# A decoder's last stage, FP4 feed-forward: three of its steps are placed on other engines and another memory

## The reference

```python
def fp4_quant_dequant(x):                       # _GRID 0 .5 1 1.5 2 3 4 6
    xb = x.reshape(shape[:-1] + (shape[-1] // BLOCK, BLOCK))
    scale = jnp.max(jnp.abs(xb), axis=-1, keepdims=True) / 6.0
    scale = jnp.maximum(scale, jnp.float32(1e-12))
    xn = xb / scale
    idx = jnp.searchsorted(_MID, jnp.abs(xn))
    q = _GRID[idx] * jnp.sign(xn) * scale
    return q.reshape(shape)
...
xl = _layernorm(x)                              # per token, 128 features
gate = fp4_linear(xl, w_gate)                   # 128 -> 352
y = fp4_linear(xl, w_up)                        # 128 -> 352
x = x + fp4_linear(jax.nn.silu(gate) * y, w_down)   # 352 -> 128
```

## Time and profile before

| | |
|---|---|
| time, median of 3 runs | 3627.68 us (3622.21 to 3630.7) |
| the profiled execution's own time | 3633.43 us |
| its span | 3631.6 us |
| mean granted TensorE clock over the span | 0.929 of full |
| busy over the span: PE, PEld, DVE, ACT, POOL | 3202.6, 2343.7, 2524.3, 2207.0, 1508.8 us |
| last stage's main block, first instruction to last of DVE | 3255.4 to 3621.4 us |

### The profile page before, as it was taken

One profiled execution on the slowest core, in us unless ns is written; L12 is line 12 of the kernel. 1 busy time (PEld: TensorE's weight loads), 2 busy tenths in 40 slices (PEclk: granted clock), 3 DMA queues, 4 the chain that ended last, 5 costly groups with the idle time before them and its releaser, 6 DMA issues. The chain is left out here.

```text
span 3631.6 us, 96279 instructions
## 1 busy us (share of the span) xinstructions
PE 3202.6 (88%) x27249; PEld 2343.7 (65%) x27249; DVE 2524.3 (70%) x7783; ACT 2207.0 (61%) x8571; POOL 1508.8 (42%) x2416
## 2 busy tenths in 40 slices
PE   8999999899999999999999731887996999977776
PEld 4656565788888888888888520665664666644444
DVE  7888888676777777777767640114666888879997
ACT  6888888566666666666666300334776999962221
POOL 6888888111111111111111125004654777746665
PEclk9999999999999999999999855999998999986666
DMA  4000000000000000000000101321000000000000
GB/s 138 0 0 0 0 0 1 4 2 3 2 2 2 2 2 2 2 2 2 2 2 2 70 9 50 84 77 30 17 16 5 6 5 5 6 3 6 12 12 18
DMA packets 80357, 54.27 MB, mean 15 GB/s; under 512 B 24801, under 2 KB 74413, under 8 KB 80160
## 3 DMA queue, kind: packets, MB, share of 16 engines
q1 hardware_dynamic: 76192, 45.27, 4.4%
q0 software_dynamic: 4096, 8.16, 0.8%
HBM read 32.67 MB, written 20.97 MB: 15 GB/s over the span
## 5 line engine op out<-in xcount | busy, mean ns | idle before, releaser
L785 DVE COPY b_prT<-b_tr 128x512 f32<-128x512 f32 x512 | 352.4, 688 | 324.3 <-PE b_tr L694 320.6
L930 POOL TENSOR_TENSOR b_ln_var<-b_ln_mean_var,all_eps 128x1 f32<-128x1 f32 x64 | 12.2, 190 | 1158.5 <-DVE b_ln_mean_var L129 1158.5
L883 ACT ACTIVATE b_pr<-b_sc,b_low 128x205 f32<-128x205 f32 x1024 | 431.2, 431 | 40.9 <-DVE b_low L761 40.9
L467 ACT ACTIVATE a_pr<-a_sc,a_low 128x128 f32<-128x128 f32 x1024 | 365.5, 384 | 36.4 <-POOL a_pn L511 26.2
L776 DVE TENSOR_SCALAR b_pn<-b_pr,b_rec 128x205 f32<-128x205 f32 x1024 | 291.6, 327 | 54.7
L694 PE MATMUL b_tr<-all_ident,b_pn 128*128 128x128 f32 x2048 | 322.4, 280 | 6.2 <-DVE b_prT L785 2.5
L2064 ACT ACTIVATE f_pr<-f_sc,f_low 128x77 f32<-128x77 f32 x1024 | 320.3, 338 | 10.2 <-DVE f_low L1955 2.9
L502 POOL TENSOR_TENSOR a_kx<-a_qk,w_hsel 128x512 f32<-128x512 f32 x256 | 291.8, 1151 | 2.4 <-DVE a_qk L338 2.4
L694 PEld LDWEIGHTS b_tr<-all_ident,b_pn 128*128 128x128 f32 x2048 | 226.5, 141 | 92.2 <-issue 69.5
L254 PE MATMUL a_sc<-a_kx,a_qk 128*128 128x512 f32 x512 | 261.9, 593 | 0.0
L761 DVE TENSOR_REDUCE b_low<-b_sc 128x4 f32<-128x820 f32 x256 | 256.3, 1001 | 6.0 <-PE b_sc L682 6.0
(11 more groups left out here) (290 smaller groups left out, 8651.3 us busy)
## 6 DMA issues: line engine op xcount, KB each, us to landing
scratch_x<-r_zeros SPq DMA_DIRECT2D x12, 512.0 KB, 5.0
e_xr<-scratch_x SPq DMA_DIRECT2D x24, 256.0 KB, 3.0
scratch_y<-e_yr SPq DMA_DIRECT2D x24, 256.0 KB, 2.4
all_X<-in_x SPq DMA_DIRECT2D x8, 512.0 KB, 7.0
e_w<-in_e_w SPq DMA_DIRECT2D x16, 256.0 KB, 3.0
out_x<-all_X SPq DMA_DIRECT2D x8, 512.0 KB, 3.2
w_mask<-in_mask SPq DMA_DIRECT2D x1, 2464.0 KB, 9.8
b_cT<-in_ctxT SPq DMA_DIRECT2D x32, 77.0 KB, 1.9
```

The lines of the kernel that those rows point to most:

```text
L467: op = act.activation(pr[:, u % 2, g], sc[:, u % 2, 128 * g:128 * g + 128], ACT.Exp, bias=low[:, u % 2, g:g + 1], scale=-1.0, accum_out=su ...
L785: dve.tensor_copy(prT[:, j % 2, i].rearrange("p h t q -> p (h t q)"), tr[:]).then_inc(prT_made, 1)
L883: op = act.activation(pr[:, j % 2, g, 0:KN], sc[:, j % 2, h, KN * i:KN * i + KN], ACT.Exp, bias=low[:, j % 2, g:g + 1], scale=-1.0, accum_ ...
```

## The change

It touches the last stage only (and adds three memsets of small constants on DVE at the kernel's start).

- One PSUM bank `pf` is allocated to the rounding: `v` and one tensor `t` for each of fx and fh lie in it. `t` takes the block maxima (k = 0) and then, in place, the reciprocals (k = 2). `v` is k = 3's output. `fp4_step` has five steps (`FP4_STEPS = 5`); k = 4, `power`, reads v from PSUM and writes SBUF. `scale` stays in SBUF.
- `magic` is formed on ACT by `fp4_magic`, in two dependent activations: Relu(power x M - M), then Identity(. + M), with M = 1.5 x 2^22, bias taken from a [128, 1] constant.
- `sum` stays on DVE as `fp4_sum`, at the end of the step, behind a wait for ACT's magic (`magic_done`).
- `norm_apply` leaves DVE: ACT's `normalise` computes xn = x * rstd + shift in one activation (bias and scale both [128, 1] operands), and POOL's `norm` computes, beside variance + eps and the power, `minus_mean` and `shift` = -mean x rstd: four instructions in the place of two.
- ACT's step is now, in order: copy_xT(b+2), gate(b+2), normalise(b+4), copy_hT(b-1), fp4_magic of fx for b+3, fp4_magic of fh for b. In the prologue it does normalise and fp4_magic of sequences 0 to 3 first, then copy_xT and gate of 0 and 1.
- In `fp4_weights` the magic constants are made on ACT likewise.

```diff
@@ -2145,25 +2145,26 @@
 
 FP4_SHRINK = 1.0 - 2.0 ** -24
 FP4_MAGIC = 1.5 * 2.0 ** 22
-FP4_STEPS = 7
+FP4_STEPS = 5
 EXPONENT_BITS = 0x7F800000
 
 class Fp4Buffers:
 
-    def __init__(self, mem, name, n):
-        nb = n // QB
-        self.amax = mem.sbuf(f"{name}_amax", [128, nb])
+    def __init__(self, mem, name, v, t):
+        n, nb = v.shape[1], t.shape[1]
+        self.v, self.t = v, t
         self.scale = mem.sbuf(f"{name}_scale", [128, 2, nb])
-        self.rscale = mem.sbuf(f"{name}_rscale", [128, nb])
-        self.v = mem.sbuf(f"{name}_v", [128, n])
         self.power = mem.sbuf(f"{name}_power", [128, n])
         self.magic = mem.sbuf(f"{name}_magic", [128, 2, n])
         self.sum = mem.sbuf(f"{name}_sum", [128, 2, n])
         self.rounded = mem.sbuf(f"{name}_rounded", [128, n])
         self.q = mem.sbuf(f"{name}_q", [128, 2, n])
         self.steps = mem.sem(f"{name}_steps")
+        self.magic_done = mem.sem(f"{name}_magic_done")
+        self.sum_done = mem.sem(f"{name}_sum_done")
         self.round_done = mem.sem(f"{name}_round_done")
         self.q_done = mem.sem(f"{name}_q_done")
 
@@ -2180,32 +2181,53 @@
 
     if k == 0:
-        if due(b - 1):
-            dve.wait_ge(f.q_done, b - 1)
-        op = dve.tensor_reduce(f.amax[:], blocks(x), AX.X, ALU.max, apply_absolute_value=True)
+        if due(b):
+            dve.wait_ge(f.steps, FP4_STEPS * b)
+        op = dve.tensor_reduce(f.t, blocks(x), AX.X, ALU.max, apply_absolute_value=True)
     else:
         dve.wait_ge(f.steps, FP4_STEPS * b + k)
     if k == 1:
-        op = dve.tensor_scalar(f.scale[:, p], f.amax[:], 1.0 / 6.0, 1e-12, ALU.mult, ALU.max)
+        if due(b - 1):
+            dve.wait_ge(f.q_done, b - 1)
+        op = dve.tensor_scalar(f.scale[:, p], f.t, 1.0 / 6.0, 1e-12, ALU.mult, ALU.max)
     if k == 2:
-        op = dve.reciprocal(f.rscale[:], f.scale[:, p])
+        op = dve.reciprocal(f.t, f.scale[:, p])
     if k == 3:
-        op = dve.tensor_tensor(blocks(f.v[:]), blocks(x), per_block(f.rscale[:]), ALU.mult)
+        if due(b):
+            dve.wait_ge(f.sum_done, b)
+        op = dve.tensor_tensor(blocks(f.v), blocks(x), per_block(f.t), ALU.mult)
     if k == 4:
-        op = dve.tensor_scalar(f.power[:].bitcast(U32), f.v[:].bitcast(U32), EXPONENT_BITS, None, ALU.bitwise_and)
-    if k == 5:
-        op = dve.tensor_scalar(f.magic[:, p], f.power[:], 1.0, FP4_MAGIC, ALU.max, ALU.mult)
-    if k == 6:
-        op = dve.scalar_tensor_tensor(out=f.sum[:, p], in0=f.v[:], scalar=FP4_SHRINK, in1=f.magic[:, p],
-                                      op0=ALU.mult, op1=ALU.add)
+        if due(b):
+            dve.wait_ge(f.magic_done, 2 * b)
+        op = dve.tensor_scalar(f.power[:].bitcast(U32), f.v.bitcast(U32), EXPONENT_BITS, None, ALU.bitwise_and)
     op.then_inc(f.steps, 1)
+def fp4_magic(act, f, consts, b, p):
+    act.wait_ge(f.steps, FP4_STEPS * b + FP4_STEPS)
+    if due(b - 1):
+        act.wait_ge(f.round_done, b - 1)
+    act.activation(f.magic[:, p], f.power[:], ACT.Relu, bias=consts.magic[:, 0:1], scale=FP4_MAGIC)\
+        .then_inc(f.magic_done, 1)
+    act.wait_ge(f.magic_done, 2 * b + 1)
+    act.activation(f.magic[:, p], f.magic[:, p], ACT.Identity, bias=consts.magic[:, 1:2]).then_inc(f.magic_done, 1)
+def fp4_sum(dve, f, b, p):
+    if due(b - 1):
+        dve.wait_ge(f.round_done, b - 1)
+    dve.wait_ge(f.magic_done, 2 * b + 2)
+    dve.scalar_tensor_tensor(out=f.sum[:, p], in0=f.v, scalar=FP4_SHRINK, in1=f.magic[:, p], op0=ALU.mult,
+                             op1=ALU.add).then_inc(f.sum_done, 1)
 
 def fp4_round(eng, f, b, p, q_read):
 
     if due(b):
         eng.wait_ge(f.q_done, b)
-    eng.wait_ge(f.steps, FP4_STEPS * b + FP4_STEPS)
+    eng.wait_ge(f.sum_done, b + 1)
     eng.tensor_tensor(f.rounded[:], f.sum[:, p], f.magic[:, p], ALU.subtract).then_inc(f.round_done, 1)
     if due(b - 1):
         eng.wait_ge(q_read, b - 1)
@@ -2246,8 +2268,14 @@
         gu_made, gated_done, h_done = mem.sem("gu_made"), mem.sem("gated_done"), mem.sem("h_done")
         hT_made, hT_copied = mem.sem("hT_made"), mem.sem("hT_copied")
         y_made, y_added, stored = mem.sem("y_made"), mem.sem("y_added"), mem.sem("stored")
-        fx, fh = Fp4Buffers(mem, "fx", D), Fp4Buffers(mem, "fh", GI)
+        pf = mem.psum("pf", [128, 512])
+        nx, nh = D // QB, GI // QB
+        fh = Fp4Buffers(mem, "fh", pf[:, 0:GI], pf[:, GI + D:GI + D + nh])
+        fx = Fp4Buffers(mem, "fx", pf[:, GI:GI + D], pf[:, GI + D + nh:GI + D + nh + nx])
         ln = NormBuffers(mem, "ln")
+        shift = mem.sbuf("shift", [128, 2])
+        minus_mean = mem.sbuf("minus_mean", [128, 2])
+        shift_done = mem.sem("shift_done")
 
@@ -2302,6 +2330,13 @@
 
             @block.scalar
             def _(act):
+                def normalise(b, p):
+                    if due(b - 1):
+                        act.wait_ge(fx.steps, FP4_STEPS * (b - 1) - 1)
+                    act.wait_ge(shift_done, b + 1)
+                    act.activation(ln.xn[:, p], X[:, b], ACT.Identity, bias=shift[:, p:p + 1],
+                                   scale=ln.rstd[:, p:p + 1]).then_inc(ln.xn_done, 1)
                 def copy_xT(b):
                     if due(b):
                         act.wait_ge(gu_made, b)
@@ -2326,9 +2361,19 @@
                     if inside(b + 2):
                         copy_xT(b + 2)
                         gate(b + 2, p)
+                    if inside(b + 4):
+                        normalise(b + 4, p)
                     if inside(b - 1):
                         copy_hT(b - 1)
-
+                    if inside(b + 3):
+                        fp4_magic(act, fx, consts, b + 3, 1 - p)
+                    if inside(b):
+                        fp4_magic(act, fh, consts, b, p)
+                for b in range(4):
+                    normalise(b, b % 2)
+                    if b < 3:
+                        fp4_magic(act, fx, consts, b, b % 2)
                 for b in (0, 1):
                     copy_xT(b)
                     gate(b, b)
@@ -2365,32 +2410,48 @@
                             residual(b - 2)
                     if inside(b + 1):
                         product(b + 1, 1 - p)
-                    if inside(b + 4):
-                        norm_apply(dve, ln, X[:, b + 4], b + 4, p)
+                    if inside(b + 3):
+                        fp4_sum(dve, fx, b + 3, 1 - p)
+                    if inside(b):
+                        fp4_sum(dve, fh, b, p)
 
                 for b in range(4):
                     norm_statistics(dve, ln, X[:, b], b, b % 2)
                     norm_moments(dve, ln, b % 2)
-                    norm_apply(dve, ln, X[:, b], b, b % 2)
                     if b < 3:
                         dve.wait_ge(ln.xn_done, b + 1)
                         for k in range(FP4_STEPS):
                             fp4_step(dve, fx, ln.xn[:, b % 2], b, b % 2, k)
+                        fp4_sum(dve, fx, b, b % 2)
                 product(0, 0)
                 over_sequences(dve, step, **steps)
 
             @block.gpsimd
             def _(pool):
+                def norm(b, p):
+                    if due(b - 1):
+                        pool.wait_ge(ln.xn_done, b - 1)
+                    pool.wait_ge(ln.moments_done, b + 1)
+                    pool.tensor_tensor(ln.var_eps[:, p:p + 1], ln.mv[:, p, 1:2], consts.eps[:, 0:1], ALU.add)\
+                        .then_inc(ln.eps_added, 1)
+                    pool.tensor_tensor(minus_mean[:, p:p + 1], ln.mv[:, p, 0:1], consts.minus_one[:, 0:1], ALU.mult)
+                    pool.wait_ge(ln.eps_added, b + 1)
+                    pool.tensor_tensor(ln.rstd[:, p:p + 1], ln.var_eps[:, p:p + 1], consts.minus_half[:, 0:1], ALU.pow)\
+                        .then_inc(ln.rstd_done, 1)
+                    pool.wait_ge(ln.rstd_done, b + 1)
+                    pool.tensor_tensor(shift[:, p:p + 1], minus_mean[:, p:p + 1], ln.rstd[:, p:p + 1], ALU.mult)\
+                        .then_inc(shift_done, 1)
                 def step(b, p, last):
                     if inside(b + 4):
-                        norm_rsqrt(pool, ln, consts, b + 4, p)
+                        norm(b + 4, p)
                     if inside(b + 3):
                         fp4_round(pool, fx, b + 3, 1 - p, xT_made)
                     if inside(b):
                         fp4_round(pool, fh, b, p, hT_made)
 
                 for b in range(4):
-                    norm_rsqrt(pool, ln, consts, b, b % 2)
+                    norm(b, b % 2)
                     if b < 3:
                         fp4_round(pool, fx, b, b % 2, xT_made)
                 over_sequences(pool, step, **steps)
@@ -2399,7 +2460,8 @@
 def fp4_weights(nc, mem, raw, wT, wdT, consts):
 
     NW = 3 * 128
-    fp4 = Fp4Buffers(mem, "w", NW)
+    pf = mem.psum("pf", [128, 512])
+    fp4 = Fp4Buffers(mem, "w", pf[:, 0:NW], pf[:, NW:NW + NW // QB])
     pt = mem.psum("pt", [128, 2, 512])
```

(7 more changed lines are left out.)

## The result

The changed kernel takes 3758.18 us (median of 4 runs, 3756.4 to 3759.44) against 3627.86 us: a ratio of 1.0354 (95%: 1.0341 to 1.0366), 130 us slower. The profiled execution has a span of 3754.6 us, where before it was 3631.6: 123.0 us more. The prediction's 104 us were a fifth too few. In the last experiment, e9_sbuf, one of twelve executions took 11435.36 us at a mean granted clock of 0.523; it is in the median given there, which would be 3634.06 us without it, and not in the ratio.

What follows compares the result with a forecast made beforehand. Two circles of one step through DVE, POOL, PE and ACT would bound the last stage; weights 3.5, prologue 13 and loop 88 us sum to 104 us slower, 3732 us, with 90% between 3668 and 3762.

Steps and rivals of the forecast that it cites:

- Circle two: Half clock, fx_sum to fx_sum through POOL, PE, ACT's gate, normalise, copy_hT, fx magic: 7.15 us, taken as 7.1.
- Circle one: Any clock, fh_sum to fh_sum through POOL's rounding and norm, normalise, copy_hT, both magics: 6.5 us, setting full-clock steps.
- that sign of the prediction: In the last stage at full clock, ACT would idle ahead of normalise, released by POOL's shift.
- The period: Last stage, between fh_sum starts: 6.9 us instead of 5.43, over 60 steps 88 us more.
- at full clock this circle is about 1.3 us shorter: Circle two at full clock would lose about 1.3 us, leaving Circle one to set 6.5 us.
- ACT's prices: Last stage, per activation: fx's magic 0.39 us, fh's 0.58, normalise 0.47.
- Relu added no table load: Rival, 3%: table loads at each Silu/Relu switch, two a step, 154 us more, 3886 us.
- Its relief: DVE's work per last-stage step would fall from 5.09 to 4.1 us, without magics, xn and fh_scale's collision.
- Prologue and weights: Before the last stage's loop: prologue 30.7 us, 13 more than before; weights 3.5 us more.
- The full clock did not hold: Rival, 20%: last stage at full clock, 6.5 us a step, 76 us slower, 3704 us.
- ACT was not cheaper: Rival, 10%: 0.28 us per 128-column activation, circles of 6.0 and 6.7 us, total 3666 to 3711 us.
- DVE was never the bound: Rival, 5%: DVE sets the last stage's period at 4.1 to 4.2 us, about 65 us faster, 3563 us.

Runs made afterwards that it cites:

- e9_sbuf: Against e8_norm_early, only the last stage's tile `pf` put back from PSUM into SBUF: 3635.84 us, ratio 1.0011 to the kernel before the change.
- e5_x_first: Against the changed kernel, only ACT's order: fx's magic ahead of the gate, fh's still last; 3721.62 us, ratio 1.0248 to the kernel before.
- e2_psum: Against the kernel before, only the PSUM bank; magic, sum and normalisation stay on DVE: 3631.78 us, ratio 0.9996.
- e8_norm_early: Against the kernel before: PSUM bank, normalisation on ACT (ahead of gate) and POOL, prologue copies and gates between normalisations, magic on DVE; 3605.33 us, ratio 0.9932.

## Why the prediction was right, and where it was off

*Circle two.* Right in its links, a little off in its size: 7.15 us by its sum (7.1 taken), 7.37 in the step shown. The stretch from copy_xT's to the gate's start was again 3.21 us. The rest is hand-overs: fx_sum's end to POOL's start 0.15 instead of 0.06, pm 0.47 instead of 0.42, pm to the copy 0.10 instead of 0.06, fx magic to fx_sum 0.10. Four small terms, 0.2 us together.

*Circle one.* Wrong as the bound of the full clock, where circle two stayed the longer. The gate stands ahead of normalise, and in nearly every step POOL's shift was there before ACT came to it: normalise waited for it 4 times in 64, 10.5 us in all; that sign of the prediction did not come. In e5_x_first, where circle two was cut, DVE and ACT closed a third circle that I had not drawn.

*The period.* 6.9 us was taken between 6.5 and 7.1; it was 7.12. This is the mis-sized term: 106.6 us where 88 stood, 1.69 us more in each of 63 steps where I had 1.47 in 60. I had mixed 6.5 us from circle one with 7.1 from circle two, by the share of the full clock. The step that failed is "at full clock this circle is about 1.3 us shorter": 1.3 us is what `pg` and `pu` save when both run at the upper level (3.21 less 1.94), and in this kernel `pu` never did, so that stretch was at most 0.3 us shorter and a step at most 0.5. But for the last three steps none is shorter than 6.80 us, so the lower figure of the mixture does not occur; the upper one is 7.39 at most. That the mean, 7.12, falls on the 7.1 us taken for half clock is in part luck: steps of 7.31 and shorter ones make it up.

*Clock.* 72% of the time at the lower level from 3300 to 3600 us, where two thirds or more were expected. The share was right; what it was taken to mean for the period was not.

*ACT's prices.* 0.39, 0.58 and 0.47 us were taken; 0.40, 0.57 to 0.59 and 0.48 were measured. One row from another stage (d_beta) and a slope between two widths were enough. Relu added no table load: one ACT_TABLE_LOAD stands in the stage, as before.

*DVE.* Its relief is real and useless in this order. The Trainium skill (SBUF — State Buffer, SBUF: two separate sides) has DVE and GpSimd lock a shared port pair for whole instructions; the trace agrees, for `fh_scale` fell from 677 to 180 ns, and in e2_psum `ln_xn`, whose operands still lie in SBUF, took 1.08 us beside POOL's rounding, where its median is 0.35. The price of the cure is on another page: by the Trainium skill (VectorE: DVE Perf Modes, Why PSUM operands drop a tier) an fp32 operand in PSUM runs at single rate. The trace agrees: fh's power went from 333 to 512 ns.

*Prologue and weights.* 30.9 and 3.3 us, expected 30.7 and 3.5.

*The rivals.* The full clock did not hold, ACT was not cheaper, and DVE was never the bound, but e8_norm_early shows how near that case was: with the magic left on DVE and the normalisation ahead of the gate it is DVE's kernel, at 4.77 us a step for most of the loop.

## What to carry to other kernels

Before work moves to an engine that looks idle, find what its idle time waits for, and draw the circle that the new work closes: an engine that takes its list in order lends time only at the places where it waits. Half a microsecond cost nothing ahead of the gate and 0.54 us a step behind it. And two edits that are worth nothing alone (the bank 0.9996, the early normalisation in SBUF 1.0011) were worth 0.7% together: test parts in pairs before a part is thrown away. A share of the time at the upper clock is no share of the steps at it: look at which matmuls on the circle ran at which level.

## What the runs showed of the hardware that was not expected

- A collision between DVE and POOL moves with their phase: freed at `fh_scale` (677 to 180 ns), it came back at `ln_xn`, in 29 of 64 instructions (1.08 us, the others 0.34).
- The full clock can be granted for 28% of the time and not reach the matmuls that a circle waits for longest: it was there while PE mostly waited, and `pu` took 0.79 us in all 128 cases, where it can take 0.46.
- A difference of 0.12 us a step at the full clock between e8_norm_early and e9_sbuf went with one of 0.52 us over the loop (4.90 against 5.42), since more steps ran at half clock, where they take 6.3 to 6.4 us. That the one difference causes the other is not shown.
